# Paired rank-1 corrections and weight loads issued one tile ahead in an attention and ternary-MLP layer on eight cores

## The chip, the cores and the metric

The kernel runs on the 8 cores of one Trainium2 chip as one program. Each core has TensorE (PE), VectorE (DVE), ScalarE (ACT), GpSimd (POOL) and the sync engine (SP), which here only issues DMAs. The metric is the device time of the slowest core, in microseconds.

## The reference

```
q = softmax((ln(x) @ Wq.T + bq) @ Wfq.T + bfq)      # over all 1024 features
k = softmax((ln(x) @ Wk.T + bk) @ Wfk.T + bfk)
v = ln(x) @ Wv.T + bv
scores = q k^T per head (16 heads of 64);  probs = scores / sum(scores)
x = x + probs @ v
x = x + bitlinear MLP(ln(x)):   gate, up: 1024 -> 4096,  down: 4096 -> 1024
weight_quant(w) = clip(round(w / mean|w|), -1, 1) * mean|w|
act_quant(x)    = per row, scale 127 / max|x|, rounded
```

x is (4, 4096, 1024) in float32. As the attention has no exp over the scores, the kernel sums k^T v over all keys of a sequence first, and multiplies it by q afterwards.

## The kernel before

Each pair of cores has one sequence. A core sweeps over all 32 tiles of 128 rows for K and V, and computes Q and the output for its own 16 (tiles 0 to 15 of its sweep). Instructions are written into one stream per engine by a planner class. Each engine carries out its stream in that order, and waits on semaphores where an entry says so. SP has its own stream, so a DMA that waits there holds all later DMAs of SP.

**Head.** Wq and Wfq are multiplied to one matrix `wcqT`, Wk and Wfk to `wckT`, and `wvT` is loaded with a transposing DMA. `emit_sum_row` and `emit_bias_row` put six rows of 1024 into `rows`, which lies on one partition: the column sums of the three matrices, and the three biases. The last row that DVE writes is the event `vRows`.

**Sweep, 32 tiles.** `emit_stats(t)` computes mean and reciprocal deviation r of an x tile (DVE, with Ln and Exp on ACT), and puts -r*mean as a row into `rm_row` (transpose on PE, L368, and copy, L371). Then tile t runs: xr = x*r (L600), eight transposes (L606), copy to `xrT` (L612), projection K into `pbA` (L544), its maximum (L618), exp to `ek_buf` with its sum (L621), reciprocal (L626), projection V into `pbV`, scaling into `vstage` (L629, L634), for own tiles projection Q into `pbA`, and the k^T v matmuls (L652). Then come the statistics of tile t+1, and for own tiles the maximum (L662), exp (L665), transposes (L671), copy (L677) and store (L681) of Q. Q's projection uses K's buffer, and so waits for K's exp.

`emit_proj` writes two halves of 512 columns. A half is 8 matmuls over the features, one matmul with one row (`rm_row` times the sum row, L550) and one with `ones_row` times the bias row (L555).

**Weight work inside the sweep.** The three MLP matrices are cut into 24 chunks of 2 MB. First pass: `emit_prep1` issues the load of a chunk from ACT's stream (L402) and right behind it the Abs activation that waits for it and adds up |w| (L404). Two chunks come at the end of each tile, from tile 0 on. Then `emit_finalize` works out the thresholds (DVE and PE, L423 to L459). Second pass: two chunks a tile, loaded one tile ahead (L479), two Sign activations each (L492, L497), an add on POOL (L510) and a store by SP (L516). `pchunk` has two buffers. The end of a tile in the loop is:

```
prep2_drain_adds(upto=p2s[0])
for _ in range(2):
    if prep_i < len(prep_chunks):
        emit_prep1(prep_i)
        prep_i += 1
    elif not fin_done[0]:
        emit_finalize()
    elif p2s[0] < p2l[0]:
        emit_prep2_signs(p2s[0])
```

**After the sweep.** All stages behind it wait for a fence over every semaphore: transposing loads of the quantized gate and up matrices, then per tile the attention output, layer norm, gate, up and SiLU, and last the down projection.

Of the kernel before, what the change touches and what calls it, by code (L numbers as in the profile page):

```python
# [9 lines left out]
BF16 = mybir.dt.bfloat16  # L10
# [5 lines left out]
D = 1024  # L16
# [60 lines left out]
def build_nc(TQ=16, TKV=32, dbg=()):  # L77
# [3 lines left out]
    p = Plan()  # L81
# [105 lines left out]
    wvT = sb(st_attn, "wvT", [128, CH * D], BF16)  # L187
    rows = sb(st_attn, "rows", [1, 6 * D], BF16)
    ROW = {n: i * D for i, n in enumerate(("wcqs", "wcks", "wvs", "bfq", "bfk", "bv"))}
    rm_row = sb(st_attn, "rm_row", [1, NKV], BF16)  # L190
    ones_row = sb(st_attn, "ones_row", [1, 128], BF16)
    ones_col = sb(st_attn, "ones_col", [128, 1], BF16)
    stat = sb(st_attn, "stat", [128, 6 * TKV], F32)
# [34 lines left out]
            bin_[n].ap().rearrange("(a d) -> a d", a=1)))  # L228
    p.op("gpsimd", lambda e: e.memset(ones_row[...], 1.0), (), "cGP", 1)
    p.op("gpsimd", lambda e: e.memset(onesf_row[...], 1.0), (), "cGP", 1)  # L230
    vGC_end = p.op("gpsimd", lambda e: e.memset(ones_col[...], 1.0), (), "cGP", 1)

    vWT = {}
# [77 lines left out]
    emit_sum_row(wckT, ROW["wcks"], [("cDV", vCk)])  # L311
    emit_sum_row(wvT, ROW["wvs"], [("dWL", vWT["wv"])])
    emit_bias_row(bk_col, wfkT, ROW["bfk"], ROW["bfk"], [])
    vRows = row_ev[-1]
    st_prek.close()
    dbg_store("rows", rows[...], [("cDV", vRows)])
# [10 lines left out]
    def emit_stats(t, vL, xsem, xap):  # L327
        c_ = STT
        vSum = dv(lambda e, t=t, xap=xap: e.reduce_sum(
            stat[:, c_["sum"] + t:c_["sum"] + t + 1], xap, axis=AX),  # L330
            waits=[(xsem, vL)])
        vSq = dv(lambda e, t=t, xap=xap: e.scalar_tensor_tensor(
            sq_scr[...], xap, 0.0, xap, op0=ALU.add, op1=ALU.mult,
            accum_out=stat[:, c_["ssq"] + t:c_["ssq"] + t + 1]), drain=True)
        dv(lambda e, t=t: e.tensor_single_scalar(
            stat[:, c_["m"] + t:c_["m"] + t + 1],
            stat[:, c_["sum"] + t:c_["sum"] + t + 1], 1.0 / D, op=ALU.mult),
            drain=True)
# [13 lines left out]
        vLn = ac(lambda e, t=t: e.activation(  # L352
            stat[:, c_["sp"] + t:c_["sp"] + t + 1],
            stat[:, c_["ssq"] + t:c_["ssq"] + t + 1], ACTF.Ln,
            bias=0.0, scale=1.0), waits=[("cDV", vVe)], drain=True)
        vR = ac(lambda e, t=t: e.activation(
            stat[:, c_["r"] + t:c_["r"] + t + 1],
            stat[:, c_["sp"] + t:c_["sp"] + t + 1], ACTF.Exp,
            bias=0.0, scale=-0.5), drain=True)
        vNR = dv(lambda e, t=t: e.scalar_tensor_tensor(  # L360
            stat[:, c_["nrm"] + t:c_["nrm"] + t + 1],
            stat[:, c_["r"] + t:c_["r"] + t + 1], -1.0,
            stat[:, c_["m"] + t:c_["m"] + t + 1],
            op0=ALU.mult, op1=ALU.mult), waits=[("cAC", vR)], drain=True)
        vNB = dv(lambda e, t=t: e.tensor_copy(
            negrm_bf[:, t:t + 1], stat[:, c_["nrm"] + t:c_["nrm"] + t + 1]),
            drain=True)
        vTr = pe(lambda e, t=t: e.transpose(  # L368
            pbtr[0:1, 0:128], negrm_bf[:, t:t + 1], identb[...]),
            waits=[("cDV", vNB), ("dX", vIb), ("cDV", evtr_state[0])])  # L370
        evtr_state[0] = dv(lambda e, t=t: e.tensor_copy(  # L371
            rm_row[0:1, t * 128:(t + 1) * 128], pbtr[0:1, 0:128]),
            waits=[("cPE", vTr)])
        stats_marks[t] = (vSq, vR)

# [14 lines left out]
    for u in range(UPW):  # L390
# [2 lines left out]
            lambda a, u=u: a[u * 128:(u + 1) * 128, :],  # L393
            lambda b, s: b[:, s * 4 * D:(s + 1) * 4 * D]))
    prep1_ac = {}

    def emit_prep1(k):
        wi, wdram, sl_, dst_ = prep_chunks[k]
        s = k % 2
        sem = ("dWP", "dWP1")[s]  # L400
        vL = dma("scalar", sem, lambda e, wdram=wdram, sl_=sl_, dst_=dst_, s=s:
                 e.dma_start(dst_(pchunk, s), sl_(wdram.ap())),  # L402
                 waits=[("cAC", prep1_ac.get(k - 2)), ("cDV", vRows)])
        prep1_ac[k] = ac(lambda e, s=s, k=k: e.activation(  # L404
            pp_buf[...], pchunk[:, s * 4 * D:(s + 1) * 4 * D], ACTF.Abs,
            bias=0.0, scale=1.0, accum_out=abscols[:, k:k + 1]),
            waits=[(sem, vL)], drain=True)

    fin_done = [False]
    prep2_i = [0]  # L410
# [56 lines left out]
    prep2_ac = {}  # L467
    prep2_ld = {}
    p2l, p2s, p2a = [0], [0], [0]
    NP2 = 3 * UPW  # L470


# [67 lines left out]
    def emit_proj(pb, XRT, wT, sum_off, bias_off, t, xw):  # L540
        vlast = None
        for h in range(2):
            for c in range(CH):
                vlast = pe(lambda e, h=h, c=c, pb=pb, XRT=XRT, wT=wT: e.matmul(  # L544
                    pb[:, 512 * h:512 * h + 512],
                    XRT[:, c * 128:(c + 1) * 128],
                    wT[:, c * D + 512 * h: c * D + 512 * h + 512],
                    start=(c == 0), stop=False),
                    waits=xw if (h == 0 and c == 0) else (), inc=False)
            vlast = pe(lambda e, h=h, t=t, sum_off=sum_off, pb=pb: e.matmul(  # L550
                pb[:, 512 * h:512 * h + 512],
                rm_row[0:1, t * 128:(t + 1) * 128],
                rows[0:1, sum_off + 512 * h: sum_off + 512 * h + 512],
                start=False, stop=False), inc=False)
            vlast = pe(lambda e, h=h, bias_off=bias_off, pb=pb: e.matmul(  # L555
                pb[:, 512 * h:512 * h + 512], ones_row[0:1, :],
                rows[0:1, bias_off + 512 * h: bias_off + 512 * h + 512],
                start=False, stop=True), inc=(h == 1))
        return vlast

    xr_dv = {}
# [29 lines left out]
    for t in range(TKV):  # L591
# [95 lines left out]

        prep2_drain_adds(upto=p2s[0])
        for _ in range(2):
            if prep_i < len(prep_chunks):  # L690
                emit_prep1(prep_i)
                prep_i += 1
            elif not fin_done[0]:
                emit_finalize()
            elif p2s[0] < p2l[0]:
                emit_prep2_signs(p2s[0])
                p2s[0] += 1
        if fin_done[0]:
            for _ in range(2):
                if p2l[0] < NP2 and p2l[0] - p2s[0] < 2:  # L700
                    emit_prep2_load(p2l[0])
                    p2l[0] += 1

    while prep_i < len(prep_chunks):
        emit_prep1(prep_i)
        prep_i += 1
    if not fin_done[0]:
        emit_finalize()
    while p2a[0] < NP2:
# [537 lines left out]
```

How the kernel before makes its waits and increments, by code:

```python
                    def body(e):  # L63
                        for fn, waits, inc, inc_by, drain in stream:
                            for sem, val in waits:
                                e.wait_ge(sems[sem], val)
                            if drain:
                                e.drain()
                            inst = fn(e)
                            if inc is not None:
                                inst.then_inc(sems[inc], inc_by)
```

## Time and profile before

| | |
|---|---|
| median of 3 runs | 2227.96 us (2224.05 to 2228.04) |
| the profiled execution | 2216.49 us |
| its span on the slowest core, core 2 | 2214.9 us |
| busy on that core | PE 65%, DVE 32%, ACT 31%, POOL 9% |
| spans of the eight cores | 2185.6 to 2214.9 us |
| mean granted TensorE clock of the cores | 0.791 to 0.799 |
| transposing loads behind the sweep begin | 1220.54 us |

All rows are of core 2. The granted clock is a share of 2.4 GHz. Lines are those of the kernel before. Busy times of an engine leave out its DMA issues and waits. "ACTq" and "SPq" are the issuing queues.

### The profile page before, as it was taken

How to read it: one execution, taken by the hardware profiler on the slowest of the kernel's cores; microseconds unless marked ns; L12 is line 12 of the kernel's file. 1: busy time of each engine (PE TensorE's matmuls, PEld its weight loads, DVE VectorE, ACT ScalarE, POOL GpSimd, SP SyncE). 2: the span in 40 equal slices, each digit the busy share in tenths (PEclk: the TensorE clock that was granted, in tenths of full speed). 3: DMA queues.
4: the chain of work that ended last, by engine and by line, in shares of the span. 5: the costliest groups of instructions: out<-in, count | busy, mean ns of one | idle time of the engine just before them, and what ended most of it. 6: DMA issues, size and time to landing. Idle time of an engine off the chain costs nothing.

```text
span 2214.9 us, 17914 instructions; the slowest of 8 cores (2185.6 to 2214.9 us)
## 1 busy us (share of the span) xinstructions
PE 1442.6 (65%) x5961; PEld 575.8 (26%) x5961; DVE 699.5 (32%) x1339; ACT 681.5 (31%) x641; POOL 200.0 (9%) x43
## 2 busy tenths in 40 slices
PE   0163667577767655545675148788888788429999
PEld 0021222222222212112222013333333333104444
DVE  0020233233232344444323215454545454201111
ACT  0000023323222545555200115555465655200000
POOL 0000000000000345555300000000000000000000
PEclk9996967767657766666666569999999999759999
DMA  8623043543533476676100971212121120474554
GB/s 120 100 41 64 1 136 134 180 147 124 180 123 148 143 251 246 247 246 247 67 19 29 186 151 43 86 44 86 44 73 56 57 73 29 91 147 130 152 153 127
DMA packets 309132, 261.34 MB, mean 118 GB/s; under 512 B 262640, under 2 KB 262768, under 8 KB 305776
## 3 DMA queue, kind: packets, MB, share of 16 engines
q10 hardware_dynamic: 144384, 132.13, 20.3%
q1 hardware_dynamic: 160160, 117.55, 17.0%
q0 software_dynamic: 4496, 10.50, 3.6%
q8 instruction: 49, 0.80, 0.1%
q14 instruction: 43, 0.35, 0.0%
HBM read 159.50 MB, written 69.21 MB: 103 GB/s over the span
## 4 chain that ended last, share of the span: by engine, by line
PE 42%; DMA 20%; ACT 10%; DVE 9%; ACTq 6%; issue 5%; DVEq 4%; SPq 4%; POOLq 0%
PE pbA L1008 8%; PE pbA L544 7%; PE pbV L1017 7%; ACTq L68 5%; PE pbV L1163 5%; PE pbA L1163 5%; DVEq L68 4%; DMA pchunk<-wg 3%; DMA pchunk<-wd 3%; DMA pchunk<-wu 3%; PE pbA L250 3%; DMA wdT<-s_dq 3%; DMA wfqT<-s_wfq 3%; ACT tq L1059 3%; PE pbV L544 2%
## 5 line engine op out<-in xcount | busy, mean ns | idle before, releaser
L1008 PE MATMUL pbA<-wgT,aq2T 128*128 128x512 bf16 x1024 | 272.1, 412 | 123.8 <-ACT silu_b L1023 54.1
L1017 PE MATMUL pbV<-wuT,aq2T 128*128 128x512 bf16 x1024 | 255.2, 393 | 38.7 <-DMA wuT<-s_uq 38.7
L510 POOL TENSOR_TENSOR pwq<-ppb,pwq 128x4096 bf16<-128x4096 bf16 x24 | 189.9, 7929 | 620.5 <-ACT pwq L497 620.5
L544 PE MATMUL pbA<-wckT,xrT 128*128 128x512 bf16 x512 | 212.0, 589 | 30.6 <-DVE xrT L612 30.6
L1031 DVE SCALAR_TENSOR_TENSOR hmid<-pbV,smal,silu_b 128x512 f32<-128x512 f32 x128 | 96.1, 750 | 321.7 <-ACT silu_b L1023 202.9
L1008 PEld LDWEIGHTS pbA<-wgT,aq2T 128*128 128x128 bf16 x1024 | 103.1, 103 | 265.6 <-issue 166.3
L1163 PE MATMUL pbA<-wdT,hqT 128*128 128x512 bf16 x512 | 125.0, 396 | 71.6 <-DMA wdT<-s_dq 71.5
L1017 PEld LDWEIGHTS pbV<-wuT,aq2T 128*128 128x128 bf16 x1024 | 104.2, 102 | 175.5 <-issue 65.9
L404 ACT ACTIVATE pp<-pchunk 128x4096 f32<-128x4096 f32 x24 | 86.8, 3617 | 168.1 <-DMA pchunk<-wg 58.7
L544 PE MATMUL pbV<-wvT,xrT 128*128 128x512 bf16 x512 | 135.0, 411 | 0.0
L1023 ACT ACTIVATE silu_b<-pbA,smal 128x512 f32<-128x512 f32 x128 | 87.9, 687 | 131.0 <-PE pbA L1008 80.3
L544 PE MATMUL pbA<-wcqT,xrT 128*128 128x512 bf16 x256 | 89.4, 513 | 53.9 <-DVE rzkb L626 53.9
L618 DVE TENSOR_REDUCE nmax<-pbA 128x1 f32<-128x1024 f32 x32 | 39.2, 1224 | 268.7 <-PE pbA L555 268.7
L1163 PE MATMUL pbV<-wdT,hqT 128*128 128x512 bf16 x512 | 111.8, 379 | 0.0
L250 PE MATMUL pbA<-wfqT,wq_nat 128*128 128x512 bf16 x128 | 31.2, 400 | 115.2 <-DMA wfqT<-s_wfq 104.9
L544 PEld LDWEIGHTS pbA<-wckT,xrT 128*128 128x128 bf16 x512 | 63.0, 133 | 159.5 <-issue 153.1
L1059 ACT ACTIVATE tq<-hmid,smal 128x1024 f16<-128x1024 f32 x64 | 73.5, 1148 | 64.2 <-DVE smal L1051 60.2
L497 ACT ACTIVATE pwq<-pchunk,bcast 128x4096 bf16<-128x4096 f32 x24 | 89.0, 3708 | 9.1 <-DMA s_gq<-pwq 7.3
L1037 DVE TENSOR_REDUCE hmx<-hmid 128x1 f32<-128x512 f32 x128 | 87.8, 686 | 11.7
L492 ACT ACTIVATE ppb<-pchunk,bcast 128x4096 bf16<-128x4096 f32 x24 | 89.0, 3708 | 2.5 <-issue 0.7
L1163 PEld LDWEIGHTS pbA<-wdT,hqT 128*128 128x128 bf16 x512 | 50.5, 99 | 144.9 <-issue 89.4
L352 ACT ACT_TABLE_LOAD x1 | 1.3, 1283 | 261.1 <-DVE stat L348 261.1
(135 smaller groups left out, 1336.7 us busy)
## 6 DMA issues: line engine op xcount, KB each, us to landing
pchunk<-wg ACTq DMA_DIRECT2D x16, 2048.0 KB, 10.5
pchunk<-wu ACTq DMA_DIRECT2D x16, 2048.0 KB, 11.0
pchunk<-wd ACTq DMA_DIRECT2D x16, 2048.0 KB, 11.6
xt_buf<-x_own SPq DMA_DIRECT2D x32, 512.0 KB, 4.9
s_hq<-hqb SPq DMA_DIRECT2D x16, 1024.0 KB, 6.5
s_gq<-pwq SPq DMA_DIRECT2D x8, 1024.0 KB, 8.3
xt_buf<-x_oth SPq DMA_DIRECT2D x16, 512.0 KB, 9.6
s_uq<-pwq SPq DMA_DIRECT2D x8, 1024.0 KB, 11.9
```

The lines of the kernel that those rows point to most:

```text
L68: e.drain()
L250: e.matmul(pbA[:, 512 * h:512 * h + 512], w_nat[:, cj * D + mi * 128: cj * D + mi * 128 + 128], wfT[:, cj * D + 512 * h: cj * D + 512 * h ...
L492: ac(lambda e, s=s, thn=thn, SGP=SGP: e.activation(SGP, pchunk[:, s * 4 * D:(s + 1) * 4 * D], ACTF.Sign, bias=bcast[:, GLO[thn]:GLO[thn] + ...
L497: vSM = ac(lambda e, s=s, nthn=nthn, PWQ=PWQ: e.activation(PWQ, pchunk[:, s * 4 * D:(s + 1) * 4 * D], ACTF.Sign, bias=bcast[:, GLO[nthn]:G ...
L510: vW = p.op("gpsimd", lambda e, SGP=SGP, PWQ=PWQ: e.tensor_tensor(PWQ, SGP, PWQ, op=ALU.add), [("cAC", prep2_ac[k])], "cGP", 1)
L544: vlast = pe(lambda e, h=h, c=c, pb=pb, XRT=XRT, wT=wT: e.matmul(pb[:, 512 * h:512 * h + 512], XRT[:, c * 128:(c + 1) * 128], wT[:, c * D ...
L1008: vG = pe(lambda e, c=c, oc=oc, gp=gp, s=s: e.matmul(gp[:, 0:512], aq2T[:, s * D + c * 128:s * D + (c + 1) * 128], wgT[:, c * DI + 512 * o ...
L1017: vU = pe(lambda e, c=c, oc=oc, up_=up_, s=s: e.matmul(up_[:, 0:512], aq2T[:, s * D + c * 128:s * D + (c + 1) * 128], wuT[:, c * DI + 512 ...
L1023: vSI = ac(lambda e, ss=ss, gp=gp, sm=sm: e.activation(silu_b[:, ss * 512:(ss + 1) * 512], gp[:, 0:512], ACTF.Silu, bias=0.0, scale=smal[: ...
L1031: e.scalar_tensor_tensor(hmid[:, oc * 512:(oc + 1) * 512], up_[:, 0:512], smal[:, sm + 6:sm + 7], silu_b[:, ss * 512:(ss + 1) * 512], op0= ...
L1059: vTQh = ac(lambda e, sl_=sl_, s=s, sm=sm: e.activation(tq16[:, s * D:(s + 1) * D], hmid[:, sl_ * D:(sl_ + 1) * D], ACTF.Copy, bias=1536.0 ...
L1163: e.matmul(pb[:, 512 * jh:512 * jh + 512], HQT[:, c * 128:(c + 1) * 128], wdT[:, c * D + 512 * jh: c * D + 512 * jh + 512], start=(c == 0) ...
```

## The change

The kernel gets a two-row left operand: `lhsT2`, row 0 as `rm_row` was and row 1 ones. `rows2` holds the three sum rows on one partition and the three bias rows on the next, copied from `rows` by two DMAs on SP's stream. One matmul with two rows takes the place of the two with one row. In the sweep, the load and the Abs of a chunk become two functions. At the end of a tile the Abs of the chunks that were loaded in the tile before come first, then the loads of the next two. The first Abs thus stands in tile 1, and finalize and all of the second pass move one tile later.

```diff
-    rm_row = sb(st_attn, "rm_row", [1, NKV], BF16)
+    lhsT2 = sb(st_attn, "lhsT2", [2, NKV], BF16)
+    rows2 = sb(st_attn, "rows2", [2, 3 * D], BF16)
...
+    p.op("gpsimd", lambda e: e.memset(lhsT2[...], 1.0), (), "cGP", 1)
     vGC_end = p.op("gpsimd", lambda e: e.memset(ones_col[...], 1.0), (), "cGP", 1)
...
     emit_bias_row(bk_col, wfkT, ROW["bfk"], ROW["bfk"], [])
+    dma("sync", "dX", lambda e: e.dma_start(
+        rows2[0:1, :], rows[0:1, 0:3 * D]), waits=[("cDV", row_ev[-1])])
+    vRows2 = dma("sync", "dX", lambda e: e.dma_start(
+        rows2[1:2, :], rows[0:1, 3 * D:6 * D]), waits=[("cDV", row_ev[-1])])
     vRows = row_ev[-1]
...
         evtr_state[0] = dv(lambda e, t=t: e.tensor_copy(
-            rm_row[0:1, t * 128:(t + 1) * 128], pbtr[0:1, 0:128]),
+            lhsT2[0:1, t * 128:(t + 1) * 128], pbtr[0:1, 0:128]),
...
-    def emit_prep1(k):
+    def emit_prep1_load(k):
         wi, wdram, sl_, dst_ = prep_chunks[k]
         s = k % 2
         sem = ("dWP", "dWP1")[s]
-        vL = dma("scalar", sem, lambda e, wdram=wdram, sl_=sl_, dst_=dst_, s=s:
-                 e.dma_start(dst_(pchunk, s), sl_(wdram.ap())),
-                 waits=[("cAC", prep1_ac.get(k - 2)), ("cDV", vRows)])
+        prep1_ld[k] = dma("scalar", sem,
+                          lambda e, wdram=wdram, sl_=sl_, dst_=dst_, s=s:
+                          e.dma_start(dst_(pchunk, s), sl_(wdram.ap())),
+                          waits=[("cAC", prep1_ac.get(k - 2)), ("cDV", vRows)])
+
+    def emit_prep1_abs(k):
+        s = k % 2
+        sem = ("dWP", "dWP1")[s]
         prep1_ac[k] = ac(lambda e, s=s, k=k: e.activation(
             pp_buf[...], pchunk[:, s * 4 * D:(s + 1) * 4 * D], ACTF.Abs,
             bias=0.0, scale=1.0, accum_out=abscols[:, k:k + 1]),
-            waits=[(sem, vL)], drain=True)
+            waits=[(sem, prep1_ld[k])], drain=True)
...
             vlast = pe(lambda e, h=h, t=t, sum_off=sum_off, pb=pb: e.matmul(
                 pb[:, 512 * h:512 * h + 512],
-                rm_row[0:1, t * 128:(t + 1) * 128],
-                rows[0:1, sum_off + 512 * h: sum_off + 512 * h + 512],
-                start=False, stop=False), inc=False)
-            vlast = pe(lambda e, h=h, bias_off=bias_off, pb=pb: e.matmul(
-                pb[:, 512 * h:512 * h + 512], ones_row[0:1, :],
-                rows[0:1, bias_off + 512 * h: bias_off + 512 * h + 512],
-                start=False, stop=True), inc=(h == 1))
+                lhsT2[0:2, t * 128:(t + 1) * 128],
+                rows2[0:2, sum_off + 512 * h: sum_off + 512 * h + 512],
+                start=False, stop=True),
+                waits=[("dX", vRows2)], inc=(h == 1))
...
         for _ in range(2):
-            if prep_i < len(prep_chunks):
-                emit_prep1(prep_i)
-                prep_i += 1
-            elif not fin_done[0]:
+            if p1a[0] < p1l[0]:
+                emit_prep1_abs(p1a[0])
+                p1a[0] += 1
+            elif p1a[0] >= len(prep_chunks) and not fin_done[0]:
                 emit_finalize()
-            elif p2s[0] < p2l[0]:
+            elif fin_done[0] and p2s[0] < p2l[0]:
                 emit_prep2_signs(p2s[0])
                 p2s[0] += 1
+        for _ in range(2):
+            if prep_i < len(prep_chunks) and prep_i - p1a[0] < 2:
+                emit_prep1_load(prep_i)
+                prep_i += 1
+                p1l[0] += 1
```

## Rows read from the trace of the kernel before

**Rows 1.** The page: the chain of waits that ended last, shares of the span by engine.

```profile
PE 42%; DMA 20%; ACT 10%; DVE 9%; ACTq 6%; issue 5%; DVEq 4%; SPq 4%; POOLq 0%
```

**Rows 2.** Busy time of each engine in two stretches: span, busy (count), clock, DMA share, GB/s.

```profile
290.00:670.00 380.00, 269.92 (x956) 92.21 (x957) 104.42 (x199) 113.75 (x100) 0.00 (x0) 0.67 0.43 153
...
2000.00:2200.00 200.00, 200.00 (x929) 90.61 (x928) 24.90 (x45) 0.00 (x0) 0.00 (x0) 1.00 0.54 150
```

**Rows 3.** Timeline, DVE's xrT copies of tiles 0, 1, 12, 13, 14, 26, 31: start, duration.

```profile
266.22 0.69 DVE L612 COPY xrT<-pbtr 128x1024 bf16<-128x1024 bf16 x1 [1.27 <-PE pbtr L606]
291.26 0.69 DVE L612 COPY xrT<-pbtr 128x1024 bf16<-128x1024 bf16 x1 [1.26 <-PE pbtr L606]
...
663.51 0.69 DVE L612 COPY xrT<-pbtr 128x1024 bf16<-128x1024 bf16 x1 [1.26 <-PE pbtr L606]
705.39 0.69 DVE L612 COPY xrT<-pbtr 128x1024 bf16<-128x1024 bf16 x1 [1.26 <-PE pbtr L606]
730.72 0.69 DVE L612 COPY xrT<-pbtr 128x1024 bf16<-128x1024 bf16 x1 [1.26 <-PE pbtr L606]
...
1076.42 0.69 DVE L612 COPY xrT<-pbtr 128x1024 bf16<-128x1024 bf16 x1 [1.26 <-PE pbtr L606]
...
1195.70 0.69 DVE L612 COPY xrT<-pbtr 128x1024 bf16<-128x1024 bf16 x1 [1.26 <-PE pbtr L606]
```

**Rows 4.** Groups of instructions, 290 to 670 us: count, busy, mean ns, idle before and releaser.

```profile
L404 ACT ACTIVATE pp<-pchunk 128x4096 f32<-128x4096 f32 x23 | 83.2, 3617 | 163.4 <-DMA pchunk<-wg 58.7 <-DMA pchunk<-wu 53.8 <-DMA pchunk<-wd 50.9
...
L626 DVE RECIPROCAL rzkb<-zkb 128x1 f32<-128x1 f32 x11 | 1.8, 164 | 90.5 <-ACT ek_buf L621 90.5
```

**Rows 5.** Timeline: ACT's first Abs of tile 6, DVE's reciprocal of tile 29.

```profile
463.92 3.62 ACT L404 ACTIVATE pp<-pchunk 128x4096 f32<-128x4096 f32 x1 [9.76 <-DMA pchunk<-wu]
...
1136.96 0.16 DVE L626 RECIPROCAL rzkb<-zkb 128x1 f32<-128x1 f32 x1 [1.40 <-ACT ek_buf L621]
```

**Rows 6.** Timeline: first Sign of four pairs, then a sign pair, POOL's adds and the cast.

```profile
726.98 3.71 ACT L492 ACTIVATE ppb<-pchunk,bcast 128x4096 bf16<-128x4096 f32 x1
...
758.26 3.71 ACT L492 ACTIVATE ppb<-pchunk,bcast 128x4096 bf16<-128x4096 f32 x1
...
793.07 3.71 ACT L492 ACTIVATE ppb<-pchunk,bcast 128x4096 bf16<-128x4096 f32 x1
...
824.25 3.71 ACT L492 ACTIVATE ppb<-pchunk,bcast 128x4096 bf16<-128x4096 f32 x1
...
962.74 3.71 ACT L492 ACTIVATE ppb<-pchunk,bcast 128x4096 bf16<-128x4096 f32 x1
...
970.38 15.81 POOL L510 TENSOR_TENSOR pwq<-ppb,pwq 128x4096 bf16<-128x4096 bf16 x2 [11.82 <-ACT pwq L497]
...
981.15 5.09 DVE L634 CAST vstage<-rzkb 128x8 bf16<-128x8 f32 x1
```

**Rows 7.** Timeline: warm halves in tile 13, the maximum of Q, and cold halves.

```profile
715.30 1.90 PE L544 MATMUL pbV<-wvT,xrT 128*128 128x512 bf16 x8
...
717.66 1.90 PE L544 MATMUL pbA<-wcqT,xrT 128*128 128x512 bf16 x8
...
722.09 0.37 PE L555 MATMUL pbA<-rows,ones_row 1*128 1x512 bf16 x1
...
724.49 1.20 DVE L662 TENSOR_REDUCE nmax<-pbA 128x1 f32<-128x1024 f32 x1
...
1125.65 3.57 PE L544 MATMUL pbA<-wckT,xrT 128*128 128x512 bf16 x8 [0.94 <-DVE xrT L612]
...
1130.11 3.59 PE L544 MATMUL pbA<-wckT,xrT 128*128 128x512 bf16 x8
```

**Rows 8.** DMA issues: KB each, median us to landing; last, all 48 loads of pchunk.

```profile
xt_buf<-x_own SPq DMA_DIRECT2D x32, 512.0 KB, 4.9
...
identb<-id_b SPq DMA_DIRECT2D x1, 32.0 KB, 1.7
...
DMA to landing us min/median/max: 7.6/10.7/16.7
```

More of the change, by code:

```diff
@@ L395, in build_nc @@
     prep1_ac = {}
-    def emit_prep1(k):
+    prep1_ld = {}
+    def emit_prep1_load(k):
         wi, wdram, sl_, dst_ = prep_chunks[k]
@@ L469, in build_nc @@
     p2l, p2s, p2a = [0], [0], [0]
+    p1l, p1a = [0], [0]
     NP2 = 3 * UPW
@@ L702, in build_nc @@
                     p2l[0] += 1
-    while prep_i < len(prep_chunks):
-        emit_prep1(prep_i)
-        prep_i += 1
+    while p1a[0] < len(prep_chunks):
+        if prep_i < len(prep_chunks) and prep_i - p1a[0] < 2:
+            emit_prep1_load(prep_i)
+            prep_i += 1
+            p1l[0] += 1
+        emit_prep1_abs(p1a[0])
+        p1a[0] += 1
     if not fin_done[0]:
```

## The prediction

> **What bounds the kernel now.** The chain of work that ended last comes first [rows 1]: TensorE (PE) has 42% of the span and DMA 20%, so no engine bounds the whole and stages must be read apart. The table by stage follows [rows 2]: in the first 12 tiles of the sweep PE is busy 269.9 of 380 us and ScalarE (ACT) 113.8, at a granted clock of 0.67. To time the tiles I take the start of the xrT copy, which stands once in each [rows 3]. I write C(t) for it.
>
> - Tile 0, the only one of these with no Abs in front of its exp of K: C(0) to C(1), 25.04 us.
> - Tiles 1 to 11: C(1) to C(12), 372.25 us, 33.84 each.
> - Tile 12, with the finalize block at its end: 41.88 us.
> - Tiles 13 to 25 (the sign pass): C(13) to C(26), 371.03 us.
> - Tiles 26 to 30, no weight work: C(26) to C(31), 119.28 us, 23.86 each.
>
> Why 33.84? ACT stands idle 163.4 us before 23 Abs instructions [rows 4], since each load is issued and awaited in the same place. In tile 6 the first Abs starts after 9.76 us of waiting for pchunk [rows 5], the second waits again, and the exp of K stands behind both. DVE's reciprocal waits 90.5 us for that exp in 11 tiles [rows 4]; where nothing is late it waits 1.40 [rows 5]. So the lateness on the path is (90.5 - 11 x 1.40) / 11 = 6.83 us a tile, and a K, V and Q tile without it takes 33.84 - 6.83 = 27.0 us. Tile 0 agrees: 25.04, one of its K and V halves at the low clock. A cold half takes 4.46 us (1125.65 to 1130.11), a warm one 2.36 (715.30 to 717.66), 2.10 apart [rows 7]; 27.0 is tile 0 with about one cold half more.
>
> **The change, part by part.**
>
> *Loads one tile ahead.* Abs instructions of a pair stay behind the exp of Q, but their loads were issued in the tile before. Are they there? The first leaves as the second Abs starts, the second as it ends, and each is wanted one tile less one Abs later: 26 - 3.8 = 22 us. The 48 loads land in 7.6 to 16.7 us, median 10.7 [rows 8], and the long ones are pairs beside stores. So both are in time. The two Abs, 7.6 us with their accumulator reads, lie between the exp of Q and the next exp of K. There stand 3.7 us of transposes and copies (726.98 to 730.72, in [rows 6] and [rows 3]), the rest of the xrT copy and its handing over (0.8), K's projection (4.7 warm, 8.9 cold [rows 7]) and its maximum (1.2): 10.4 to 14.6. This cover hides them; were it gone they would cost 7.6 a tile, 91 us in 12 tiles. Tiles 1 to 12 go from 33.84 to 27.0.
>
> *One tile later.* Abs of chunks 22 and 23 moves to tile 12's end, so finalize stands in tile 13, the sign pass in tiles 14 to 25, and the plain tail is one tile shorter. Finalize costs 11.7 us (41.88 less 27.0 is 14.9; I leave 3.2 of it to tile 12's own late exp, so 11.7; at 14.9 the sum grows by 3).
>
> *Sign pass.* Its cycle is not PE's. From sign pair to sign pair 27.6 us pass: C(26) less the 3.7 us from signs to C, less 824.25, over 9. Of them 7.6 go by to the start of GpSimd (POOL)'s adds (962.74 to 970.38), 15.81 with the two adds, the DVE cast of 5.09 us ends with them (986.2) [rows 6], and what is left, 4.2, is the statistics that the next signs stand behind. Projections lie beside it, so fewer matmuls save nothing there. The first sign pairs stand at 726.98, 758.26, 793.07 and 824.25 [rows 6]: 31.28 for a Q tile without a store wait, 34.81 for one with it, 31.18 for a K, V tile with it. Shifted, the stage has one Q tile fewer: C(14) to first signs 21.6 - 0.9 = 20.7; 31.28; 31.18; the stretch 824.25 to 1076.42, 252.2, as it is; one cycle more, 27.6. Sum 363.0, against 371.0.
>
> *Rank-1 matmuls.* Two of 10 matmuls per half become one: 160 fewer. A warm half of ten takes 2.36, so 0.236 each; a cold one 0.446 [rows 7]. If the low clock (0.50 of 2.4 GHz, where a half takes 4.46) ends at a point of time whatever was issued until then, what is left out shortens the warm rest, so I take the warm price. Q's projection ends at 722.46 in tile 13 and DVE turns to it at 724.49 [rows 7], so its two are free; K's and V's four are on the path: 4 x 0.236 = 0.94 us a tile, 20 tiles (0 to 14, 27 to 31), 18.9 us. At the cold price: 36. The free two would cost up to 0.9 a tile if DVE's cover went. A two-row operand costs no more than one row as I take it: full 128-row matmuls have the same spacing in these rows. The first lhsT2 memset (4096 elements on two partitions) stands on POOL behind its first DMAs and far ahead of its reader, the sum row behind eight combines; even at some microseconds it is hidden.
>
> *Two row copies on SP's queue.* This is the loss. Before, x tiles 0 and 1 wait for no row and are in SBUF early, and DVE goes from the last row straight to tile 0's statistics. Now SP waits for that row, issues copy one, waits for it (same semaphore), copy two, waits, then loads x(0); x(1) and everything later on SP queue behind it, and DVE, PE and ACT all wait for x(0). No SBUF to SBUF row copy stands in this trace. Bounds for one, by the nearest rows: 1.7 (identb, 32 KB) and 4.9 (an x tile, 512 KB) [rows 8]; a copy has 6 KB, so I take 2.2, near the first. x(0): 4.9, the median of x_own [rows 8]. 2 x 2.2 + 4.9 + 0.5 of issuing = 9.8 us; from 8.8 to 15.2. The Trainium skill, "DMA: Bandwidth & Descriptors", section "Anatomy of one DMA", gives a fixed 2.0 us per DMA plus bytes; by that the copies cost 4.0 and the term is 9.4. No row here shows it for such a copy.
>
> **Sum.** Tiles 0 to 13 after: 24.1 + 12 x 26.06 + 26.06 + 11.7 = 374.6, before (0 to 12) 439.2: -64.6. Sign stage -8.0. Tail: 4 x 22.92 = 91.7 against 119.3: -27.6. Tile 31: -0.9. Head: +9.8. Total -91.3. Everything behind the sweep (weight transposes behind the fence, both MLP stages) starts from its end and moves as a block. The profiled execution took 2216.5, so 2125; the median of the runs shown is 2228.0, 11.5 above it, so **2137 us**.
>
> Bounds of the likeliest case: Q tiles from 25.0 to 29.2 (one or three cold halves) are -24 to +26 in 12 tiles, hardly all to one side; rank-1 at the cold price -17; head -1 to +5. I take 2110 to 2162.
>
> **Rivals.**
>
> *Loads still late.* The pair is issued almost together and shares the 16 engines with x and eqT. A load leaves behind the Abs before it, so the tile can't be shorter than landing plus 3.8. At 26 us (above every row's 16.7) it is 29.8 in place of 26.1: +45, 2182. For: in the first stage each load was alone and still took up to 12.2. Against: in the sign pass a pair with stores beside it fits in 27.6. Chance 0.11.
>
> *Warmer than counted.* PE no longer pauses before Q. If the clock stays high across tiles, Q tiles go to 24.1, below all I took, and 24 us more fall away, with some in the tail: 2105. Against: the pause between tiles, with nothing but small transposes in it, stays. Chance 0.07.
>
> *Slower: both loads starve.* All eight cores now read 4 MB at one time, and loads that ran apart run together. Loads served one after the other, each at 18.7 us, 2 above the longest row, make a tile of 37.4, 11.3 above 26.1: +136, 2273. It decides from a tile of 33.7 (12 x 7.6 = 91), that is a pair of 4.2 MB at 125 GB/s. Against: the first stage already moves 153 GB/s on average [rows 2]. Chance 0.03.
>
> *The change doesn't do what it says.* The wait moves to the second stage's store or to SP, and the Abs wait shows as before; what is left is rank-1 (-18.9), head (+9.8) and one Q tile at 33.8 more for the 8.0 and 23.9 that the shift gives back (+1.9): 2221, at the edge of 0.2%. The rows give no such wait. Chance 0.02.
>
> *Lower clock under dense work.* In the last stage PE is busy 200 of 200 us at a granted clock of 1.00, the 2.4 GHz level, on this of eight working cores [rows 2]. The Trainium skill, "TensorE: Matmul & The Clock Gate", section "Architectural detail: the array is 16× 32×32, not 1× 128×128", tells of a limiter at 13/16 once three cores of a die are dense; the row disagrees. As a mechanism of this kernel: a warm half a quarter longer, +0.5 us, two such on the path in 20 tiles, +20: 2157, inside the range. Chance 0.01.
>
> **How the numbers follow.** Likeliest 0.76, the others as given. Range 2105 to 2168: it leaves out about half of the late loads, the slower rival, the null, and the far tails of the first. About 0.2% (4.5 us) is what a measurement can tell from no change. Faster 0.95 (likeliest, late loads, warmer, lower clock), same 0.02, slower 0.03.
>
> **What would show it.** Right: no DMA wait of Abs; the first reciprocals wait 1.4 us; C(t) 24 to 28 us apart in tiles 1 to 12; finalize in tile 13; sign cycle still 27.6; rows L550 with 2-row operands, 160 in all; C(0) near 276. Wrong: ACT idle before Abs on pchunk, Q tiles above 29, or C(0) beyond 281. The prediction falls if K, V and Q without the wait are bound by something its length hid.

## The result: 6% faster, by more than the forecast

The changed kernel takes **2097.0 us** (median of 10 runs, 2093.3 to 2135.0) against 2228.0 us, a ratio of **0.942** (95% interval 0.940 to 0.944). The forecast was 2137 us, and the time lies 8 us below the range. Of 91 us forecast, 131 came. In some executions the cores of one die show a lower granted clock and the time is some per cent longer: medians and ranges include them, ratios leave them out.

The page of the profile after is of core 7 (span 2095.2 us, its execution 2096.8). First its busiest engines and the chain by engine, which answers [rows 1]:

```profile
PE 1316.1 (63%) x5801; PEld 556.4 (27%) x5801; DVE 706.2 (34%) x1339; ACT 683.0 (33%) x641; POOL 203.4 (10%) x44
...
PE 42%; ACT 12%; DVE 12%; DMA 11%; ACTq 8%; DVEq 5%; issue 4%; SPq 4%; POOL 0%; POOLq 0%
```

DMA had 20% of the chain before and has 11% now. The other shares moved by at most 3 points. The stages, with the columns of [rows 2], are tiles 1 to 11, most of the sign pass, and the plain tiles at the end:

```profile
296.00:569.00 273.00, 195.50 (x869) 79.46 (x869) 103.67 (x199) 108.31 (x98) 0.00 (x0) 0.78 0.63 199
660.00:990.00 330.00, 154.46 (x640) 61.74 (x639) 149.15 (x184) 188.72 (x93) 188.97 (x25) 0.70 0.66 233
1000.00:1070.00 70.00, 45.11 (x193) 17.32 (x193) 26.00 (x53) 6.04 (x14) 0.00 (x0) 0.78 0.05 16
```

In the first stage (on the slowest core of each execution) the granted clock rose from 0.67 to 0.78, and the DMA rate from 153 to 199 GB/s. The Abs waits are gone, as the groups of the same stage show (they answer [rows 4]), and DVE's reciprocal waits 1.40 us, exactly the undisturbed wait of [rows 5]:

```profile
L416 ACT ACTIVATE pp<-pchunk 128x4096 f32<-128x4096 f32 x23 | 83.2, 3617 | 2.1 <-issue 0.4
...
L636 DVE RECIPROCAL rzkb<-zkb 128x1 f32<-128x1 f32 x12 | 2.0, 164 | 16.8 <-ACT ek_buf L631 16.8
```

The starts of the xrT copies answer [rows 3]: C(0), C(1), C(12), C(13), C(14), C(27) and C(31).

```profile
270.19 0.69 DVE L622 COPY xrT<-pbtr 128x1024 bf16<-128x1024 bf16 x1 [1.26 <-PE pbtr L616]
295.66 0.69 DVE L622 COPY xrT<-pbtr 128x1024 bf16<-128x1024 bf16 x1 [1.26 <-PE pbtr L616]
...
568.75 0.69 DVE L622 COPY xrT<-pbtr 128x1024 bf16<-128x1024 bf16 x1 [1.26 <-PE pbtr L616]
593.39 0.69 DVE L622 COPY xrT<-pbtr 128x1024 bf16<-128x1024 bf16 x1 [1.26 <-PE pbtr L616]
...
629.77 0.69 DVE L622 COPY xrT<-pbtr 128x1024 bf16<-128x1024 bf16 x1 [1.26 <-PE pbtr L616]
...
995.66 0.69 DVE L622 COPY xrT<-pbtr 128x1024 bf16<-128x1024 bf16 x1 [1.26 <-PE pbtr L616]
...
1076.85 0.69 DVE L622 COPY xrT<-pbtr 128x1024 bf16<-128x1024 bf16 x1 [1.26 <-PE pbtr L616]
```

Held beside the terms of the forecast, in us:

| stretch | before (core 2) | forecast | after (core 7) |
|---|---|---|---|
| C(0) | 266.2 | 276.0 | 270.2 |
| tiles 0 to 12, after: 0 to 13 | 439.2 | 374.6 | 359.6 |
| sign pass, C(13) to C(26), after: C(14) to C(27) | 371.0 | 363.0 | 365.9 |
| plain tiles, each | 23.9 | 22.9 | 20.3 |
| plain tiles, 5 and then 4 | 119.3 | 91.7 | 81.2 |
| C(31) | 1195.7 | 1105.3 | 1076.9 |
| behind C(31) to the end of the span | 1019.2 | as before | 1018.3 |

Tiles 1 to 11 come 24.8 us apart (568.75 less 295.66, over 11), against 26.1 forecast. The 40 us between 2137 and 2097.0 come from three places. 25.5 lie in the plain K, V and Q work (15.0 in tiles 0 to 13, 10.5 in the plain tiles), the part that hangs on TensorE's clock. 5.8 lie in C(0), and the sign pass takes 2.9 back. The last 11.5 aren't in the traces at all: the forecast added them because the median before lay that far above the profiled execution, and after the change the two are 0.2 apart. Why they were apart before stays open. For the rest of this document a tile length is the mean over the eight cores of a profiled execution, from the same copies.

The head shows the new wait. SP issues the two row copies 1.9 us apart, x follows 1.7 us later, and DVE stands idle until it is there:

```profile
255.60 1.21 DVE L289 CAST rows<-pbV 1x1024 bf16<-1x1024 f32 x1 [4.56 <-PE pbV L285]
```

That is the last row in the kernel before, 10.6 us ahead of its C(0). The kernel after, from its last row on:

```profile
252.16 1.21 DVE L291 CAST rows<-pbV 1x1024 bf16<-1x1024 f32 x1 [4.56 <-PE pbV L287]
253.52 0.64 SPq L316 DMA_DIRECT2D rows<-rows  x1
255.39 0.50 SPq L318 DMA_DIRECT2D rows<-rows  x1
257.09 0.81 SPq L586 DMA_DIRECT2D xt_buf<-x_own  x2
260.69 1.22 DVE L335 TENSOR_REDUCE stat<-xt_buf 128x1 f32<-128x1024 f32 x1 [7.32 <-DMA xt_buf<-x_own]
```

The wait is 7.32 us, where the forecast had 9.8. From the last row to C(0) it is now 18.0 us. But the last row itself comes 3.4 us earlier than it did on core 2, so C(0) moved by 4.0 only.

### The profile page after: what moved, and what is told of

The parts are those of the page before. It is cut to its first block, busy times and chain, and to the rows that moved or that the text cites. A ratio compares the mean times of both kernels' runs of the same rounds, so it can differ in the third digit from the quotient of the medians.

```text
span 2095.2 us, 17600 instructions; the slowest of 8 cores (2078.5 to 2095.2 us)
## 1 busy us (share of the span) xinstructions
PE 1316.1 (63%) x5801; PEld 556.4 (27%) x5801; DVE 706.2 (34%) x1339; ACT 683.0 (33%) x641; POOL 203.4 (10%) x44
## 3 DMA queue, kind: packets, MB, share of 16 engines
q10 hardware_dynamic: 144384, 132.13, 22.9%
## 4 chain that ended last, share of the span: by engine, by line
PE 42%; ACT 12%; DVE 12%; DMA 11%; ACTq 8%; DVEq 5%; issue 4%; SPq 4%; POOL 0%; POOLq 0%
PE pbA L1027 8%; ACTq L68 8%; PE pbV L1036 7%; PE pbA L557 5%; PE pbV L1182 5%; DVEq L68 5%; PE pbA L1182 5%; PE pbV L557 4%; DMA wdT<-s_dq 3%; DMA wfqT<-s_wfq 3%; PE pbA L252 3%; ACT tq L1078 3%; ACT hqb L1082 2%; SPq L825 2%; ACT pwq L510 2%
## 5 line engine op out<-in xcount | busy, mean ns | idle before, releaser
L557 PE MATMUL pbA<-wckT,xrT 128*128 128x512 bf16 x512 | 181.4, 517 | 30.6 <-DVE xrT L622 30.6
L557 PE MATMUL pbV<-wvT,xrT 128*128 128x512 bf16 x512 | 121.6, 380 | 0.0
L662 PE MATMUL pbK<-vstage,ek_buf 128*128 128x129 bf16 x256 | 24.7, 251 | 115.5 <-DVE vstage L644 115.5
L631 ACT ACTIVATE ek_buf<-pbA,nmax 128x1024 bf16<-128x1024 f32 x32 | 35.6, 1114 | 176.6 <-DVE nmax L628 170.1
L557 PEld LDWEIGHTS pbA<-wckT,xrT 128*128 128x128 bf16 x512 | 56.7, 121 | 131.6 <-issue 113.5
L358 ACT ACTIVATE stat<-stat 128x1 f32<-128x1 f32 x32 | 6.5, 203 | 252.1 <-DVE stat L354 252.1
```

## Experiments

### Only the loads ahead

The one-row matmuls stay, and there are no row copies.

```diff
+ load and Abs of a chunk apart, as in the change
- lhsT2, rows2, the two row copies, the merged matmul
```

> Only the loads one tile ahead; the two one-row matmuls per half stay, and there are no row copies. Theory A (the pause in front of Q's projection kept TensorE at its low clock, so taking the pause away shortens the cold stretches by itself): tiles 1 to 12 come 25.6 us apart (the changed kernel's 24.7 and 0.9 for the rank-1 matmuls), the last tiles keep the two kinds seen before (20.7 on some cores, 23.9 on others), about 2116 us. Theory B (the cold stretches got shorter because of the merged matmuls): tiles 1 to 12 stay at the forecast 27.0 us, the last tiles as before, about 2134 us. Tile 0 starts some 7 us earlier than in the changed kernel under both.

Measured: **2149.7 us** (2139.3 to 2163.0), ratio 0.961 (0.953 to 0.969). Tiles 1 to 11: 26.95 us, on single cores 26.5 to 27.2. The last four tiles: 23.1 on average, 20.7 to 24.2 by core. Theory A falls and theory B stands. One half of theory A holds: the pause did keep Q's own matmuls at the low level. From the first to the last of Q's 16 feature matmuls it was 6.7 us before and is 4.3 now (mean of eight cores, tiles 1 to 11). It shortens no tile, for K keeps its long low stretch, 8.2 us from its first matmul to V's first before and 7.9 now.

The forecast had 27.0 us for this tile with its one-row matmuls. Its total for this kernel can be read from its own terms, 2137 + 18.9 - 9.8 = 2146 us, 4 us from what came. So what was forecast about the loads came as a sum, and the miss is in the merge. The sum was helped by luck. The tile fell by 6.8 us, and the lateness of K's exp accounts for it (6.9 on the mean core). But two terms that the forecast left out are nearly as large as each other: the transpose of -r*mean stood 1.9 us behind Q's matmuls before and 0.1 now, and the scaling into `vstage` now waits 2.15 us for V, for which it never waited before.

Two kinds of last tile show in the granted clock of single cores. Here are a stretch of them in the kernel before (cores 0 and 2) and one in this kernel (cores 1 and 3):

```profile
core 0: us, PE busy (x) PEld busy (x) DVE busy (x) ACT busy (x) POOL busy (x), PEclk, DMA share, GB/s
1085.00:1175.00 90.00, 56.95 (x254) 21.79 (x255) 32.24 (x67) 7.64 (x18) 0.00 (x0) 0.77 0.05 18
...
core 2: us, PE busy (x) PEld busy (x) DVE busy (x) ACT busy (x) POOL busy (x), PEclk, DMA share, GB/s
1085.00:1175.00 90.00, 59.76 (x215) 20.60 (x215) 30.42 (x64) 6.44 (x16) 0.00 (x0) 0.65 0.05 18
```

```profile
core 1: us, PE busy (x) PEld busy (x) DVE busy (x) ACT busy (x) POOL busy (x), PEclk, DMA share, GB/s
1020.00:1095.00 75.00, 49.72 (x217) 18.29 (x215) 26.69 (x53) 6.03 (x14) 0.00 (x0) 0.77 0.04 15
...
core 3: us, PE busy (x) PEld busy (x) DVE busy (x) ACT busy (x) POOL busy (x), PEclk, DMA share, GB/s
1020.00:1095.00 75.00, 52.02 (x181) 17.37 (x181) 22.82 (x48) 4.84 (x12) 0.00 (x0) 0.66 0.05 15
```

At 0.77 a core runs these tiles in 20.7 us, at 0.65 in 23.9 to 24.2. Before, five of eight cores were of the slow kind, and the slowest core sets the time.

### Only the merge

```diff
+ lhsT2, rows2, the two row copies, the merged matmul
- load and Abs of a chunk apart
```

> Only the merged two-row matmul with its row copies; loads and Abs as before. Theory A: the Abs waits stay, tiles 1 to 11 stay near 33 us and the last tiles keep both kinds on different cores; with 0.9 us less in the tiles without another bound and 7 us more ahead of tile 0, about 2214 us. Theory B: all eight cores run the last five tiles at 20.3 us in place of 23.9, and the first tiles lose more than 0.9 each: 2195 us or less.

Measured: 2215.0 us (2187.9 to 2228.1), ratio 0.987 (0.976 to 0.997). That comparison is unclear: the median is theory A's number, the profiled execution, 2187.9 us, is on theory B's side, and the interval is too wide to tell. The trace is clearer. All eight cores run the last four tiles at 20.4 us (20.2 to 20.6). Tiles 1 to 11 take 32.4, against 33.8, although the Abs wait is still there and the exp of K is later than ever:

```profile
L410 ACT ACTIVATE pp<-pchunk 128x4096 f32<-128x4096 f32 x22 | 79.6, 3617 | 150.4 <-DMA pchunk<-wu 54.9 <-DMA pchunk<-wg 54.7 <-DMA pchunk<-wd 40.8
...
L629 DVE RECIPROCAL rzkb<-zkb 128x1 f32<-128x1 f32 x11 | 1.8, 164 | 110.8 <-ACT ek_buf L624 110.8
```

The reciprocal waits 110.8 us in 11 tiles, 20.3 more than in [rows 4]. Projections are done sooner, and the Abs pair is not: from the copy of xrT to that reciprocal it is 18.7 us in both kernels (mean of eight cores). What these tiles win, 15.1 to 13.7 us, lies behind it, where Q's projection stands. Theory B again, by the tiles: the merge alone takes the slow kind of last tile away.

### Is it the number of matmuls, or their rows?

First the merged matmul with 128 rows, 126 of them zeros:

```diff
-    lhsT2 = sb(st_attn, "lhsT2", [2, NKV], BF16)
-    rows2 = sb(st_attn, "rows2", [2, 3 * D], BF16)
+    lhsT2 = sb(st_attn, "lhsT2", [128, NKV], BF16)     # rows 2 to 127 zero
+    rows2 = sb(st_attn, "rows2", [128, 3 * D], BF16)   # rows 2 to 127 zero
...
-                lhsT2[0:2, t * 128:(t + 1) * 128],
-                rows2[0:2, sum_off + 512 * h: sum_off + 512 * h + 512],
+                lhsT2[:, t * 128:(t + 1) * 128],
+                rows2[:, sum_off + 512 * h: sum_off + 512 * h + 512],
```

> The changed kernel with 128 rows in the merged matmul (126 of them zeros), so that its number is the same and every matmul of a half uses all rows. If the number of rows of the correction matmul has a say in the granted clock, the cold stretches get shorter still and the last tiles fall below 20 us: 2085 us or less. If only the number of matmuls and the pauses count: 2097 us within 4 us, tiles as in the changed kernel.

**2086.4 us** (2083.8 to 2087.7), ratio 0.935 (0.931 to 0.940). Tiles 1 to 11: 23.91 us, 0.85 less than in the changed kernel; the last tiles 20.12, the same. So rows do count for the time, by more than the 4 us allowed for, but 1.4 us short of the 2085 that the other theory asked for, and its last tiles didn't fall below 20. That the clock gained by it is not shown: a half at the high level takes 1.94 us here and 2.15 in the changed kernel (both below), and by these, as an estimate, the four halves of K and V are 0.84 shorter, which is the whole difference. Then ten matmuls in each half, all with 128 rows:

```diff
+            pe(lambda e, h=h, sum_off=sum_off, pb=pb: e.matmul(
+                pb[:, 512 * h:512 * h + 512], zeros128[...],
+                rows2[:, sum_off + 512 * h: sum_off + 512 * h + 512],
+                start=False, stop=False), ...)
```

> Ten matmuls in each half again, as in the kernel before, but all ten with 128 rows: the 128-row correction matmul and one more with an operand of zeros (its sum is unchanged). Theory R (what keeps the clock low is that two of ten matmuls have one row only): the last tiles come about 20.5 us apart on every core, tiles 1 to 12 at 23.9 + 0.9 = 24.8 us, 2105 us. Theory N (ten matmuls instead of nine are what keeps it low, whatever their rows): tiles 1 to 12 at 27.0, the last tiles of two kinds (20.7 and 23.9), about 2145 us.

**2097.1 us** (2096.6 to 2098.5), ratio 0.941. Tiles 1 to 11: 24.69 us. The last tiles: 20.4, on no core above 20.9. As many matmuls as with the loads alone, and 2.3 us a tile less. The number is not the cause; theory R stands by its tiles, though the time is 8 us below the 2105 that it was given. The timelines of one late K, V tile show how. First the loads alone (ten matmuls in a half, two of one row), core 7:

```profile
1053.99 3.57 PE L551 MATMUL pbA<-wckT,xrT 128*128 128x512 bf16 x8 [0.94 <-DVE xrT L619]
1058.45 3.59 PE L551 MATMUL pbA<-wckT,xrT 128*128 128x512 bf16 x8
1062.94 3.59 PE L551 MATMUL pbV<-wvT,xrT 128*128 128x512 bf16 x8
1066.80 0.38 PE L562 MATMUL pbV<-rows,ones_row 1*128 1x512 bf16 x1
1067.11 1.90 PE L551 MATMUL pbV<-wvT,xrT 128*128 128x512 bf16 x8
1069.17 0.37 PE L562 MATMUL pbV<-rows,ones_row 1*128 1x512 bf16 x1
```

then this kernel (ten, all of 128 rows), core 7:

```profile
1035.33 3.57 PE L561 MATMUL pbA<-wckT,xrT 128*128 128x512 bf16 x8 [0.94 <-DVE xrT L631]
1039.40 1.89 PE L561 MATMUL pbA<-wckT,xrT 128*128 128x512 bf16 x8
1041.56 1.89 PE L561 MATMUL pbV<-wvT,xrT 128*128 128x512 bf16 x8
1043.71 1.89 PE L561 MATMUL pbV<-wvT,xrT 128*128 128x512 bf16 x8
1045.66 0.38 PE L572 MATMUL pbV<-rows,lhsT 128*128 128x512 bf16 x1
```

and the changed kernel (nine, one of two rows), core 7:

```profile
1036.90 3.57 PE L557 MATMUL pbA<-wckT,xrT 128*128 128x512 bf16 x8 [0.94 <-DVE xrT L622]
1040.40 0.60 PE L563 MATMUL pbA<-rows,lhsT 2*128 2x512 bf16 x1
1040.94 2.07 PE L557 MATMUL pbA<-wckT,xrT 128*128 128x512 bf16 x8
1043.26 1.90 PE L557 MATMUL pbV<-wvT,xrT 128*128 128x512 bf16 x8
1045.41 1.90 PE L557 MATMUL pbV<-wvT,xrT 128*128 128x512 bf16 x8
1047.24 0.38 PE L563 MATMUL pbV<-rows,lhsT 2*128 2x512 bf16 x1
```

A line of 3.57 or 3.59 us is eight matmuls at the low level (0.50 of 2.4 GHz), one of 1.90 is eight at the high. With two one-row matmuls in a half, both halves of K and the first of V run at the low level, 13.1 us (1053.99 to 1067.11). In the other two the clock has risen by the end of K's first half (ten matmuls of 128 rows) or early in its second (the changed kernel). What stands right ahead is the same in all three: the transposes of x, which end 1 us before K.

The lines also price a warm half: 2.16 us with ten matmuls of 128 rows (1039.40 to 1041.56), 2.15 with eight and one of two rows (1043.26 to 1045.41), and 2.36 with eight and two of one row [rows 7]. At 0.216 each (2.16 over ten), nine matmuls would be 1.94 us and ten 2.16; both halves with short matmuls lie 0.20 to 0.21 above that. (The run with nine matmuls of 128 rows shows its 1.94 in V, 351.68 to 353.62 on core 5.) So going from 128 rows to few and back costs some 0.2 us a half, whether one or two matmuls of few rows stand between, and 128 rows are cheaper than two. This is an estimate from these lines; no run prices the two changes apart.

### One row against two

```diff
-                lhsT2[0:2, ...], rows2[0:2, ...]          # merged
+                rm_row[0:1, ...], rows[0:1, ...]          # mean correction alone
- the row copies
```

> Loads one tile ahead, and nine matmuls in each half, the ninth with one row; the bias rows (all zero in these inputs) are left out of K, V and Q, and with them the row copies and the second row. Both theories: tiles 1 to 12 near 24.7 us as in the changed kernel, one kind of last tile; what it tells is whether one row or two matter. If the second row counts, tiles come out longer than 25.2. 2093 us within 6.

**2096.3 us** (2091.3 to 2147.6), ratio 0.940. Tiles 1 to 11: 24.75, to be held beside 24.76; last tiles 20.24. The second row has no say, and neither have the row copies, which this kernel lacks. This half has as many changes of row count as the half with two one-row matmuls, and one such matmul fewer. So those changes alone don't keep the clock low; what the long tiles have besides is the second matmul of few rows.

### Eight matmuls

```diff
- both correction matmuls
-                    start=(c == 0), stop=False),
+                    start=(c == 0), stop=(c == CH - 1)),
```

> Loads one tile ahead, and only the eight 128-row matmuls in each half: mean correction and bias are left out of K, V and Q. It prices the ninth matmul. Theory R: as the 128-row run (23.9 us) less 4 x 0.236 = 0.9: tiles 1 to 12 at 23.0, the last tiles at or below 20.4, and no copies: about 2065 us. If the last tiles do not get shorter although a matmul is gone, their length is set by where the clock rises and not by the number of matmuls.

**2071.7 us** (2067.8 to 2073.1), ratio 0.930, where about 2065 was expected. The last tiles fell to 18.95 us. Tiles 1 to 11 stayed at 23.84, where 23.0 was expected; K's two halves take 6.07 us here (339.51 to 345.58 on core 1), and 5.92 with 18 matmuls of 128 rows (345.76 to 351.68 on core 5). What was left out came back in good part as a longer stretch at the low level. Why here and not in the last tiles stays open.

### The head

```diff
+    vX0_early = dma("sync", "dX", lambda e: e.dma_start(
+        xt_buf[:, 0:D], x_own.ap()[0:128, :]))
+    vX1_early = dma("sync", "dX1", ...)              # tile 1
     dma("sync", "dX", lambda e: e.dma_start(rows2[0:1, :], ...
```

> The changed kernel with the first two x loads issued ahead of the two row copies, so that statistics of tile 0 need not wait behind them. If the term for the head (forecast 9.8 us, read from the trace after as about 7.4) is what this order costs, tile 0 starts 6 to 8 us earlier and the time is 2090 us. If the copies' own landing holds the first projection instead, less than 2 us come back: 2095 to 2097 us.

**2096.8 us** (2093.4 to 2121.0), ratio 0.940 (0.934 to 0.945): the wait is gone from the trace, and no gain from the time. So both kernels ran once more side by side, the changed one and this one:

> The changed kernel unaltered, to be held beside the next one on the same chip: 2097 us within 5, tile 0's statistics waiting 7 us for x.

> The first two x loads ahead of the row copies, on the chip of the run before. The trace said 7.3 us less of waiting ahead of tile 0, the first timing (2096.8 us) said nothing. If what is won at the head reaches the end, 2090 us, 0.3% below the run before; if the slowest core's later stages take it back, both lie within 0.1%.

2099.1 us (2090.8 to 2119.7) and 2097.0 us (2090.7 to 2106.1), ratios 0.944 and 0.944. In four profiled executions the mean C(0) of the eight cores is 268.8 and 268.2 without, 265.2 and 267.0 with the early loads; the mean of the spans 2086.2 and 2085.8, and 2083.9 and 2084.4. About 2 us reach the average core, and the slowest core's time can't tell it.

Why so little of 7.3 us? Because the last row moves the other way. Means of eight cores, from the same traces: with x behind the copies it starts at 250.3 to 251.4 us (five executions: the changed kernel twice, the merge alone, nine and ten matmuls of 128 rows), with x early at 254.4 to 256.4 (the other eight, the kernel before among them). The two early x loads are issued at about 12 us, among the loads of the head's weights, and 1 MB more moves there. That they hold the weights back is likely and not shown; that the edit costs 4 to 6 us at the last row is what both pairs of executions show (250.7 to 254.5, 250.3 to 256.4).

### The sign pass, and a version that beats both

The sign pass was the one stage that no part of the change touches. Its cycle of 27.6 us had a small DVE copy in it that stood still behind GpSimd [rows 6]. On top of the 128-row matmul and the early x loads:

```diff
-        vS2 = dv(lambda e, s=s, VST=VST: e.tensor_copy(
-            VST...[:, :, 128:129], rzkb...broadcast_to([128, NPAIR, 1])))
+        vS2 = dv(lambda e, s=s, VST=VST: e.tensor_scalar(
+            VST...[:, :, 128:129], pbV...[:, :, 0:1],
+            0.0, rzkb[:, s:s + 1], op0=ALU.mult, op1=ALU.add))
```

> The 128-row correction and the x loads first, and in it the small DVE cast into vstage, which stood still until both GpSimd adds were done (5.09 us in place of 0.17), reads the projection's PSUM buffer times zero plus the reciprocal instead of SBUF. If the standstill belongs to this form of copy, the sign cycle becomes ScalarE's: 15.2 for four signs, 1.3 exp, 0.3, 1.3 vstage, 0.2 cast, 4.2 statistics, 0.6, near 23.1 in place of 27.6 us, twelve times: about 2030 us. If the statistics behind it (two reads of x from SBUF) stand still in its place, the cycle stays at 27.6 and the time near 2082 us.

**2069.0 us** (2064.8 to 2125.6), ratio 0.928 (0.924 to 0.932). Neither end: the cycle is 26.3 us on most cores. In the timeline the copy runs at once, and then so does the sum; the sum of squares, which reads x twice from SBUF, stands still until the adds end at 882.5 and its own work is done:

```profile
866.72 15.82 POOL L529 TENSOR_TENSOR pwq<-ppb,pwq 128x4096 bf16<-128x4096 bf16 x2 [11.55 <-ACT pwq L516]
877.50 0.24 DVE L653 TENSOR_SCALAR vstage<-pbV,rzkb 128x8 bf16<-128x8 f32 x1
877.63 1.21 DVE L341 TENSOR_REDUCE stat<-xt_buf 128x1 f32<-128x1024 f32 x1
878.93 4.70 DVE L344 SCALAR_TENSOR_TENSOR sq_scr<-xt_buf 128x1024 f32<-128x1024 f32 x1
```

4.70 us in place of 1.22. Then the statistics by another instruction:

```diff
-        reduce_sum, scalar_tensor_tensor (x*x, summed), three small operations
+        for hh in range(2):
+            vSq = dv(... e.bn_stats(bnb[:, 6 * hh:6 * hh + 6],
+                                    xap[:, 512 * hh:512 * hh + 512]))
+        dv(... e.bn_aggr(mv[:, 2 * t:2 * t + 2], bnb[...]))
```

> The kernel of cast_psum, and in it the statistics of a tile by two bn_stats of 512 elements and a bn_aggr in place of the sum, the sum of squares and three small operations. The squares had taken over the standstill behind GpSimd's adds (4.70 us in place of 1.22). If bn_stats, with one input from SBUF, does not stand still, the sign cycle loses 3.5 us of it and 1 to 2 us of work in each of 12 tiles (26.3 to about 22), every other tile 1 to 2 us, together about 2000 us. If it stands still too, only the shorter work is won, near 2040 us. If bn_stats costs more than the two operations that it replaces (above 1.2 us for each 512), it is slower than 2069.

**2024.5 us** (2019.8 to 2060.0), ratio **0.910** (0.907 to 0.913), the fastest of all. Tiles 1 to 11: 22.56 us, the last ones 18.2. In the sign pass bn_stats runs beside the adds without a stop, and ACT now waits for DMA, both for a chunk and for the store of one:

```profile
850.07 3.71 ACT L504 ACTIVATE pwq<-pchunk,bcast 128x4096 bf16<-128x4096 f32 x1 [2.66 <-DMA s_dq<-pwq]
853.92 15.82 POOL L517 TENSOR_TENSOR pwq<-ppb,pwq 128x4096 bf16<-128x4096 bf16 x2 [9.12 <-ACT pwq L504]
865.03 1.28 DVE L343 BATCH_NORM_STATS2 bnb<-xt_buf 128x6 f32<-128x512 f32 x2
866.41 0.21 DVE L346 BATCH_NORM_AGGREGATE mv<-bnb 128x2 f32<-128x12 f32 x1
869.02 3.71 ACT L499 ACTIVATE ppb<-pchunk,bcast 128x4096 bf16<-128x4096 f32 x1 [1.54 <-DMA pchunk<-wd]
876.64 3.71 ACT L504 ACTIVATE pwq<-pchunk,bcast 128x4096 bf16<-128x4096 f32 x1 [3.91 <-DMA s_dq<-pwq]
```

So the cycle is 25.8 us (mean of eight cores, the last ten tiles of the pass) and not 22. ACT's waits in it are now for transfers; that these set the cycle was not tested.

## Why the prediction was wrong

**Range missed, mechanism of the loads right in the main.** The Abs waits went from 163.4 us to 2.1, lateness of K's exp to nothing, and the two Abs fitted under K's projection. The pairs of loads landed in time; the median of all 48 rose from [rows 8] to this, and the longest, 18.9, came in the first pass, with 21.0 available in a tile of 24.8 (22 was forecast):

```profile
DMA to landing us min/median/max: 9.8/12.6/18.9
```

The tile of 27.0 us, taken from the lateness alone, came as 26.95 once the merge was kept out, in part by luck: two left-out terms of some 2 us cancel, as said above. Finalize kept its price (36.38 us for tile 13, 11.6 above its neighbours). It moved to tile 13, the sign pass to tiles 14 to 25, and its cycle stayed at 27.6; of the 2.9 us above its forecast 1.7 are one tile of 32.9 in place of 31.2, the rest small excesses. The stages behind the sweep moved as a block.

**The step that failed** is the price of the rank-1 matmuls, "4 x 0.236 = 0.94 us a tile, 20 tiles, 18.9 us". The warm price itself was near: a warm half fell from 2.36 to 2.15 us, 0.84 for the four. What failed is the condition it stood on, that the low clock "ends at a point of time whatever was issued until then". The runs show otherwise. With the one-row pairs the low stretch at the start of K goes on for one or two halves more; a half at the low level costs 2.1 us. Measured: 26.95 - 24.76 = 2.19 us in each of tiles 1 to 11, and 23.1 - 20.2 = 2.9 in each of the last four. Less the 0.84, a shorter low stretch gives some 1.35 and 2.1 us a tile, for which the forecast had nothing. Between the kernel with the loads alone and the changed one, C(31) falls by 39 us on the average core (1110.8 to 1071.8) and by 50 on the slowest (1126.4 to 1076.9); the medians by 52.7, with the row copies paid, where the forecast's own terms give 18.9 - 9.8 = 9.1. By the ratios, each against the kernel before on its own chip, it is some 42.

**Where the rivals stand.** "Warmer than counted" was the right direction (Q tiles at 24.8 for its 24.1), for the wrong reason: it put the clock down to the pause before Q, and without that pause, with the one-row pairs, only Q's own halves got warmer and no tile shorter than counted. It was priced at 24 us and given 0.07. Late loads, starved loads and a lower clock under dense work did not show; the granted clock of the eight cores went from 0.79 to 0.82, and in the last stage (1950 to 2050 us) it is 1.00 on all eight. The limiter at 13/16 that the prediction cites from the Trainium skill, "TensorE: Matmul & The Clock Gate", stands there in the section "Seeing it yourself", not in the one it names; these traces don't show it. "The change doesn't do what it says" fell with the first row.

**The tail** was forecast from core 2, which is of the slow kind. A look at the other cores would have shown three of eight at 20.7 us with the same instructions, that is a clock with two outcomes for one stream of work, and a size for what a small push could win: 3.1 us in each of five tiles.

**The head** was sized at 9.8 us and is 7.3 as a wait; row copies take 1.9 and 1.7 us from issue to issue, near the lower bound. They are near the 2.0 us, too, that the prediction cites from the Trainium skill, "DMA: Bandwidth & Descriptors", section "Anatomy of one DMA — SWDGE (gpsimd) path"; but that section is about DMAs that GpSimd issues, and these two come from SP. The term also left something out: x is no longer loaded early, and the last row comes 4 us sooner. C(0) rose from 265.4 to 268.8 us on the mean core, 3.4 in place of 9.8.

**The 11.5 us** between median and profiled execution were carried from before to after without a reason that the rows show. They did not recur, and are over a quarter of the miss.

**What was shown and what not.** Shown: ten matmuls of 128 rows give the short tiles, eight with two of one row the long ones, eight with one of one or two rows the short ones. The table has the six kernels with the loads ahead; K is from its first matmul to V's first, means of eight cores.

| matmuls in a half | tiles 1 to 11 | K in them | last four tiles | K in them |
|---|---|---|---|---|
| 8 of 128 rows, 2 of one row | 26.95 | 7.9 | 23.1 | 8.2 |
| 8 of 128 rows, 1 of two rows | 24.76 | 6.2 | 20.2 | 6.2 |
| 8 of 128 rows, 1 of one row | 24.75 | 6.2 | 20.2 | 6.2 |
| 10 of 128 rows | 24.69 | 6.2 | 20.4 | 6.3 |
| 9 of 128 rows | 23.91 | 5.7 | 20.1 | 6.4 |
| 8 of 128 rows | 23.84 | 6.0 | 18.95 | 5.7 |

Not shown: how the clock is decided. That it weighs the rows at work is the reading that fits the first four; that what counts is the time spent on matmuls of few rows, or two of them in a row, fits as well, and no run separates these.

## What to carry to other kernels

Where a kernel's TensorE clock moves between its two levels, price an edit of its matmuls at both, and at what it may do to the level itself. Look at the same tile on all cores: two lengths for one stream of instructions were the sign here that a small change can tip it. Look too at what an early load stands among before it is moved. A rank-1 correction is not small because it has one row. Fold such rows into one matmul, and give it all 128 rows where SBUF allows.

## What the runs showed that was not expected

- A warm half of ten matmuls takes 2.16 us when all have 128 rows, and 2.36 when two have one row. Padding with zeros is faster than two rows: 2086.4 against 2097.0 us.
- The granted clock of one stream differed between cores of one execution, 0.77 and 0.65, tile after tile.
- While GpSimd adds (7.9 us each), a DVE copy of 128 x 8 from SBUF takes 5.09 us, and a product of two SBUF reads 4.70 in place of 1.22. The same values by way of PSUM took 0.24 us, a sum over 1024 elements of one SBUF tile 1.21, and bn_stats 1.28 for two, beside the same adds.
